# The last batches of a sort by indirect DMA: four, two and one chunk instead of five and two

## What is computed

```
xn = layernorm(x)
gnn[n] = sum over edges e with src[e] == n of edge_weight[e] * xn[dst[e]]
mix = second-order attention of xn (8 heads of 32, q, k, v from Wqkv), then Wproj
x = x + gnn + mix
x = x + ffn(layernorm(x))     # top 2 of 16 experts, 256 -> 512 -> 256, then a layernorm
```

## Time and profile before

| | us |
|---|---|
| median of 3 runs | 2158.93 |
| lowest, highest | 2154.53, 2159.85 |
| profiled execution | 2159.11 |
| its span, first to last instruction | 2157.3 |

### The profile page before, as it was taken

One profiled execution on the slowest core, in us unless ns is written; L12 is line 12 of the kernel. 1 busy time (PEld: TensorE's weight loads), 2 busy tenths in 40 slices (PEclk: granted clock), 3 DMA queues, 4 the chain that ended last, 5 costly groups with the idle time before them and its releaser, 6 DMA issues.

```text
span 2157.3 us, 41674 instructions
## 1 busy us (share of the span) xinstructions
PE 1852.7 (86%) x11902; PEld 1251.0 (58%) x11950; DVE 1407.6 (65%) x3497; ACT 1128.4 (52%) x3220; POOL 1317.4 (61%) x1258
## 2 busy tenths in 40 slices
PE   5676767899999999799999999987756999999940
PEld 3454553555555555445455444445756898999940
DVE  8999998887777777455555566765663444433347
ACT  4765653454444445365665666654632444455434
POOL 2233435777777777777777777772773666544434
PEclk8688987899999999999999999997558999999975
DMA  5333101333333333333333343385764555555565
GB/s 189 109 130 129 30 27 36 99 99 100 101 101 100 100 100 101 105 113 111 113 113 111 113 123 111 113 101 134 241 226 94 99 101 101 102 104 106 103 198 217
DMA packets 150077, 248.13 MB, mean 115 GB/s; under 512 B 25312, under 2 KB 109410, under 8 KB 149922
## 3 DMA queue, kind: packets, MB, share of 16 engines
q0 software_dynamic: 64496, 144.32, 27.8%
q1 hardware_dynamic: 82466, 99.36, 14.6%
q10 hardware_dynamic: 2960, 2.57, 0.4%
HBM read 182.25 MB, written 63.91 MB: 114 GB/s over the span
## 4 chain that ended last, share of the span: by engine, by line
PE 54%; POOL 15%; DVE 12%; issue 8%; DMA 7%; ACT 3%; SPq 0%; DVEq 0%; POOLq 0%; ACTq 0%
POOL big L855 12%; PE b L1955 10%; PE bqk L2237 8%; PE bank L2217 8%; DMA big<-xn_dram,big 5%; PE bank L2093 4%; PE bqk L2104 3%; POOL z_dram L864 3%; PE bqk L2009 2%; PE b L1971 2%; PE bank L1900 2%; PE b L2207 1%; PE bank L1985 1%; PE bqk L1882 1%; DVE st L1235 1%
## 5 line engine op out<-in xcount | busy, mean ns | idle before, releaser
L855 POOL DMA_INDIRECT big<-xn_dram,big x832 | 828.9, 996 | 255.4 <-issue 230.1
L1955 PE MATMUL b<-big 128*128 128x256 f32 x1468 | 395.6, 394 | 29.8 <-DMA big<-xn_dram,big 27.0
L1955 PEld LDWEIGHTS b<-big 128*128 128x128 f32 x1468 | 259.2, 191 | 197.8 <-issue 102.8
L884 POOL DMA_INDIRECT sum_dram<-mid,idxy x113 | 176.4, 1561 | 227.4 <-DMA sum_dram<-mid,idxy 124.9
L998 ACT ACTIVATE big<-big 128x128 f32<-128x128 f32 x832 | 265.7, 403 | 37.2 <-DVE big L1465 18.9
L2217 PEld LDWEIGHTS bank<-late,mid 128*128 128x128 f32 x1808 | 219.4, 193 | 9.8 <-issue 5.0
L2217 PE MATMUL bank<-late,mid 128*128 128x128 f32 x1808 | 223.2, 277 | 0.0
L2237 PE MATMUL bqk<-big,mid 128*128 x896 | 215.7, 384 | 0.0
L1490 DVE TENSOR_TENSOR acc<-acc,b 128x256 f32 x251 | 104.9, 418 | 154.3 <-PE b L1955 118.5
L1069 ACT ACTIVATE big<-bank 128x512 f32<-128x512 f32 (+1 forms) x208 | 102.3, 577 | 165.5 <-PE bank L2093 165.5
L2237 PEld LDWEIGHTS bqk<-big,mid 128*128 128x128 f32 x896 | 161.2, 190 | 20.7 <-issue 0.2
(11 more groups left out here) (348 smaller groups left out, 3356.6 us busy)
## 6 DMA issues: line engine op xcount, KB each, us to landing
big<-w SPq DMA_DIRECT2D x32, 512.0 KB
mid<-z_dram SPq DMA_DIRECT2D x114, 130.0 KB, 2.1
mid<-b SPq DMA_DIRECT2D x113, 128.0 KB, 3.4
big<-xn_dram,big POOLq DMA_INDIRECT x832
sum_dram<-mid SPq DMA_DIRECT2D x19, 640.0 KB, 4.0
big<-sum_dram SPq DMA_DIRECT2D x18, 640.0 KB, 13.1
acc<-x_pad SPq DMA_DIRECT2D x10, 640.0 KB, 6.6
xn_dram<-big SPq DMA_DIRECT2D x9, 640.0 KB, 3.4
```

What stands on the lines that cost most here:

```text
L855: pool.indirect_dma_start(out=gx[t % GB], out_offset=None, in_=xn_dram, in_offset=bass.IndirectOffsetOnAxis(ap=dstA[:, t:t + 1], axis=0)). ...
L884: pool.indirect_dma_start(out=sum_dram[t % 2], in_=yo[t % 4], in_offset=None, out_offset=bass.IndirectOffsetOnAxis(ap=idxy[t % 4][:, 0:1], ...
L1955: a = pe.matmul(to[:, 0:C], wd[t % (2 * EB)], gx[t % GB], start=(e == unit[0] and j == 0), stop=(e == unit[-1] and j == 1), skip_group_che ...
```

## The change

`BEND` ends with 46, 48, 49 instead of 47, 49. So batch 6 is chunks 42 to 45 (before, 42 to 46), batch 7 is chunks 46 and 47 (before, 47 and 48), and there is a batch 8 with chunk 48 alone. `places` runs nine times, behind chunks 45, 47 and 48 at the end. Its wait ahead of the index write is for 46 moves in batch 8, for 42 in batch 7. Of the batch before the last one move is held back until the last fetch is issued: GpSimd's order at the end is moves 42 to 45, fetches 46 and 47, move 46, fetch 48, moves 47 and 48, tail. Before, it was moves 42 to 44, fetches 47 and 48, moves 45 to 48, tail.

```diff
-BEND = [7, 14, 21, 28, 35, 42, 47, 49]
+BEND = [7, 14, 21, 28, 35, 42, 46, 48, 49]
             for m in range(last):
                 fetch_batch(m)
-                for c in range(BEND[m - 1] if m else 0, BEND[m] - (2 if m == last - 1 else 0)):
+                for c in range(BEND[m - 1] if m else 0, BEND[m] - (1 if m == last - 1 else 0)):
                     move(c)
             fetch_batch(last)
-            for c in range(BEND[last - 1] - 2, NCH):
+            for c in range(BEND[last - 1] - 1, NCH):
                 move(c)
```

## The result

The changed kernel takes 2166.01 us (median of 13 runs, 2161.25 to 2168.17), the kernel before 2158.23 us in the 13 runs beside it (2150.65 to 2159.85). The ratio is 1.0036, with a 95% interval of 1.0026 to 1.0045: slower by 7.8 us, where 3.6 us was forecast. The profiled execution of the changed kernel has a span of 2164.2 us, 6.9 more than before. The change was to bring the last moves forward. It does so for moves 42 to 46 (move 42 comes 3.5 us earlier), but VectorE then stands and waits for one of them, and the last two moves come 1.0 and 1.1 us later than before.

What follows compares the result with a forecast made beforehand. GpSimd's row of gathers bounds the kernel, its start set by VectorE's path: +5.9 - 1.2 = +4.7 us at the first edges, less 1.1 slack = +3.6, so 2159.1 + 3.6 = 2162.7 us. Range: 2157.5 to 2167 us.

Steps and rivals of the forecast that it cites:

- What bounds the kernel: GpSimd's L855 gathers, 378.0 to 1461.0 us, run without real pause; VectorE's path decides their start: d late moves them d - 1.1 us.
- Smaller batch 6 and third table: End of the sort: move 42 issues 4.0 us earlier; the extra table adds 1.4 us of VectorE work at the index write.
- The new wait: VectorE at the last table: stands 4.4 us for the 46th move, index write at 342.2 instead of 336.29, +5.9 us.
- GpSimd behind it: GpSimd after move 45: late chunk 48 fetch gives back the 4.0 us; first L846 at 359.75, own path gains 0.9 us.
- What comes back in the unpacking: VectorE's 13-block unpacking: fewer long L1463 shifts beside L846 issues give back some 1.2 us, bounds 0 and 1.6.
- (A): Last table: new wait not met; gathers move by -0.9 to 0, 2158.2 to 2159 us; chance 0.15 with partial forms.
- (B): First edge matmuls: TensorE's clock rises behind the L2009 preceding pair 2; +7.2 us, 2166.3 us; chance 0.12.
- (C): Faster: the earlier move 42 reaches the gathers, or a different phase of later waits gives over 6.5 us; chance 0.04.
- (D): No unpacking gain and a long issue in the moves: +5.9 us, 2165.0 us; chance 0.09 with a little more.

Runs made afterwards that it cites:

- the three buffers: Changed kernel with three index buffers instead of two, so the last table waits for 42 moves, not 46: 2156.79 us, ratio 1.0001 to the kernel before.
- the early release of chunk 48: Changed kernel with VectorE releasing chunk 48 to TensorE ahead of its table, not behind it: 2163.89 us, ratio 1.0034 to the kernel before.

## Why the prediction was right, and where it was too small

*What bounds the kernel* held. The shift of gather 16 (5.8 us) is still 5.7 at the last one, and the slack of 1.1 us between the two paths is there: pair 2 moved by 6.9, gather 16 by 5.8. The agreement to 0.1 us is luck in part: from gather 16 to the last one the two traces of the kernel before take 1062.6 and 1063.6 us, those of the changed kernel 1062.5 and 1060.5. That a lead of GpSimd brings nothing while VectorE's path stays is shown from both sides, by the three buffers (GpSimd 3.6 us ahead, no gain) and by the early release of chunk 48 (3.2 us ahead of the changed kernel, no gain), both counted from the first fetch of batch 6.

*Smaller batch 6 and third table.* Move 42 was reckoned 4.0 us earlier and came 3.5 earlier; the table of chunk 45 ended at 317.4 (317.5 reckoned). VectorE was even earlier at the last table than reckoned, 337.1 against 337.7.

*The new wait* was the right mechanism, 4.4 us of idle time reckoned, 6.4 measured, and 6.2 to 6.8 us on the index write (from the table above, 17.4 or 18.0 less 11.2) where 5.9 was reckoned. The step that failed is the even pace of the moves: 3.05 us a move was taken from two steps of the kernel before, and the first step took 3.9 to 4.25 us in the two traces of the changed kernel. That is 0.8 to 1.2 us. The rest of the 2 us of extra idle time is VectorE's being 0.6 us early, which costs nothing, and batch 6 starting 0.5 us later in this trace, less 0.4 us by which move 45's landing was reckoned too late behind its issue.

*GpSimd behind it.* The first block of records was reckoned at 359.75 and came at 360.76, as late as the moves and fetch 48 were. It had room.

*What comes back in the unpacking* is the second mis-sized term: 1.2 us reckoned, 0.3 measured between the first two traces (59.9 to 59.6). The one row at 379.77 misled me into thinking that L1463 is only held by L846. The trace of the kernel before already had a row against it, for only five of its six long shifts meet an L846 issue; the sixth falls into the first gather. Its timelines of VectorE and GpSimd:

```profile
378.52 0.44 DVE L1463 TENSOR_SCALAR big<-rpk 128x64 int32<-128x64 int32 x1
```

```profile
378.00 0.95 POOL L855 DMA_INDIRECT big<-xn_dram,big  x1 [0.30 <-issue]
```

In the changed kernel's timelines of the unpacking:

```profile
378.48 0.20 DVE L1463 TENSOR_SCALAR big<-rpk 128x64 int32<-128x64 int32 x1
...
386.78 0.44 DVE L1463 TENSOR_SCALAR big<-rpk 128x64 int32<-128x64 int32 x1
...
390.54 0.44 DVE L1463 TENSOR_SCALAR big<-rpk 128x64 int32<-128x64 int32 x1
```

```profile
386.26 0.95 POOL L855 DMA_INDIRECT big<-xn_dram,big  x1 [0.30 <-issue]
```

The L1463 of 386.78 ends at 387.22, the issue of an L855 at 387.21. So it is long during L855 too. By the rule of the Trainium skill ("GPSIMD Engine Reference", Key points) that I had set aside, VectorE's instructions in a 2-port mode contend with GpSimd; no run here shows whether this shift is in such a mode. The traces agree with it in part: five of the 13 shifts here are held, but those that start 0 to 0.4 us into an issue stay short. How many of the 13 are long depends on how the two rhythms fall, 3 to 11 in the traces above. Eight times 0.24 us is 2 us, and the moment of the clock's rise adds up to 1 us; the whole stretch differs by up to 3.4 us from one trace to another (58.8 to 62.2). A margin of some 2 us either way should have stood in the range for the unpacking, in place of 0 to 1.6.

*The rest.* With both terms corrected (+0.9 for the moves, +0.9 for the unpacking) the sum is 5.4 us, and the traces show 5.7 at the last gather. The end of the profiled execution is 1.2 us later still, behind the gathers, and the medians differ by 7.8 us (5.6 to 9.7 by the interval). From the last gather to the end the two traces of the kernel before take 696.3 and 694.5 us, those of the changed one 697.5 and 695.7, so single traces can't settle it. Whether the missing two microseconds are a cost or spread is open: the same stall without new batches gave 6.3 us, with the early chunk 48 7.3 us, and all three intervals overlap.

*The rivals.* (A), no stall, didn't come. (B), the clock, didn't come between the first two traces. Busy times of two stretches of the changed kernel, then granted clock, DMA share and GB/s:

```profile
395.00:398.00 3.00, 2.26 (x7) 1.36 (x7) 2.34 (x6) 2.53 (x10) 1.69 (x2) 0.50 0.26 68
398.00:401.00 3.00, 3.00 (x13) 0.84 (x12) 2.94 (x5) 2.63 (x9) 1.75 (x3) 0.71 0.24 74
```

The rise falls near 399.7 us (0.71 is 1.7 us at 1.2 GHz and 1.3 at 2.4), 6.8 later than before, as the work did. But (B)'s mechanism is real in a small form, in both kinds of kernel: in the second trace of the kernel before, the rise is late and pair 2 comes 0.9 us later behind pair 0 (10.4 us against 9.5), and where move 42 waits for the fetches the projection takes 3.61 us, not 2.78. It needs no change of the batches. (C) didn't come. (D), no gain from the unpacking and a long move, is nearest to what happened: I had priced it at +5.9 and given it 0.09. I had given slower by over 0.3% a chance of 0.18; the measured 0.36%, with its interval of 0.26 to 0.45, is on that side, and a fair chance would have been nearer to a half. The time lies in the range, but above the forecast's own spread of 2160 to 2165, and what takes the range up to 2167 is (B), which didn't make this time: that part is luck.

## What to carry to other kernels

Before an engine's work is brought forward by cutting batches smaller, look at every wait that counts in batches: with two buffers, one more and shorter batch makes its wait later in the count (here from 42 moves to 46), and it can fall on the engine that sets the time. Here a stall behind such a wait cost about its length (7.8 us for 6.4, and 6.3 for 6.6); the slack of 1.1 us took its part off only where the other path didn't stand behind the same wait. A third small buffer took the loss away. And a pace read from two steps of a chain needn't hold for its other steps: price the chain with its worst step in the trace as well. Last, when single traces are compared, count from a common event just ahead of the change: the place of the whole sort differed by up to 3.1 us here (first fetch of batch 6 at 323.17 to 326.29).

## What the runs showed of the hardware

A shift of VectorE of 0.20 us (L1463, int32, 128x64) takes 0.44 us when it starts 0.52 to 0.53 us into a GpSimd issue of an indirect DMA of 0.95 us, and ends with the issue. In the eleven traces 74 of the 143 shifts started there and 69 of them were long; none of the others was. Five stayed short in that place too, the one at 379.77 us in the kernel before among them, each in the second gather; why isn't shown. The issue of an indirect DMA takes 0.94 to 1.1 us mostly, 1.2 to 1.6 us in others, and 1.8 to 2.3 us now and then, often at the same instruction when a kernel is run again (2.2 us at the third move of batch 5, in both traces of both kernels, but 1.1 us there in the kernel before with one move held back, whose GpSimd program is the same up to that point). What lengthens it isn't shown.
